# Products of attention chances and values for two steps at a time, over a ring of six pairs of chances

## The reference

```
h = layernorm(x) * (1 + ca) + sa
q, k, v = split(h @ W_qkv.T + b_qkv)            # 16 heads of 16
scores = q k^T * 16**-0.5, causal (-inf above the diagonal)
attn = softmax(scores); out = attn @ v; x = x + ga * (out @ W_out.T + b_out)
h = layernorm(x) * (1 + cb) + sb
cw = group-limited top-4 weights of softmax(h @ gate_w.T)   # 16 experts
x = x + gb * (sum_e cw[:, e] * swiglu_e(h) + swiglu_shared(h))
```

## Time and profile before

| what | us |
|---|---|
| median of 3 runs | 717.92 (717.07 to 720.73) |
| the profiled execution's own time | 718.91 |
| its span, first to last instruction | 716.9 |
| TensorE busy over the span | 626.2 (87%) |
| VectorE busy | 523.8 (73%) |
| ScalarE busy | 392.6 (55%) |
| GpSimd busy | 321.3 (45%) |
| products L2005 busy | 83.6, 768 matmuls |
| first score to last product | 94.9 to 397.7 |

### The profile page before, as it was taken

The page is one execution under the profiler, slowest core; times in us unless marked ns, Lnnn a source line. Parts: engine busy times, 40 slices in busy tenths (PEclk is TensorE's granted clock), DMA queues, the critical chain, the costliest instruction groups (busy, mean ns, idle before and its releaser), DMA issues. The chain is left out here.

```text
span 716.9 us, 13724 instructions
## 1 busy us (share of the span) xinstructions
PE 626.2 (87%) x3946; PEld 412.2 (58%) x3946; DVE 523.8 (73%) x1466; ACT 392.6 (55%) x919; POOL 321.3 (45%) x511
## 2 busy tenths in 40 slices
PE   2959879898999998978977989778999999999967
PEld 2747433334343434443423767567778888888756
DVE  4899978878788786857775687857886556555558
ACT  4446256666666656555686544436855455555440
POOL 4535533616142225327187874714973343434400
PEclk9979879999999999977999899989999999999979
DMA  8249957713030403032042435728333333333277
GB/s 277 90 141 277 351 165 203 198 37 105 16 99 23 119 2 100 21 128 105 31 148 76 147 129 189 248 88 288 103 105 121 105 107 120 107 120 107 75 300 299
DMA packets 65020, 98.03 MB, mean 137 GB/s; under 512 B 12115, under 2 KB 49747, under 8 KB 64693
## 3 DMA queue, kind: packets, MB, share of 16 engines
q1 hardware_dynamic: 56788, 73.10, 33.1%
q0 software_dynamic: 6864, 19.01, 7.0%
q10 hardware_dynamic: 1296, 5.05, 2.0%
HBM read 52.77 MB, written 42.14 MB: 132 GB/s over the span
## 5 line engine op out<-in xcount | busy, mean ns | idle before, releaser
L1261 ACT ACTIVATE Pr<-bank 128x512 f32<-128x512 f32 (+3 forms) x384 | 166.2, 494 | 99.3 <-PE bank L2019 94.2
L2019 PE MATMUL bank<-Qs,Ks 99*128 99x512 bf16 (+3 forms) x384 | 123.6, 344 | 16.0 <-ACT Pr L1261 10.4
L1915 PE MATMUL bank<-Ks,Qs 96*128 96x512 bf16 (+3 forms) x384 | 126.4, 348 | 6.5 <-DVE mxB L1382 5.3
L1382 DVE TENSOR_REDUCE mxA<-bank 128x1 f32<-128x128 f32 (+3 forms) x256 | 113.0, 485 | 25.4 <-PE bank L1915 24.9
L1094 POOL DMA_INDIRECT expert_rows<-Y,YIX x79 | 77.0, 975 | 116.3 <-DVE YIX L1802 84.2
L1078 POOL TENSOR_TENSOR tick<-ident 128x1 f32<-128x1 f32 x128 | 26.2, 204 | 179.3 <-ACT Pr L1261 178.7
L1382 DVE TENSOR_REDUCE mxB<-bank 128x1 f32<-128x512 f32 x128 | 82.0, 683 | 17.0 <-PE bank L1915 16.5
L2239 PE MATMUL bank<-W,xh 128*128 x316 | 84.3, 349 | 3.4 <-issue 3.4
L2005 PE MATMUL bank<-Pr,Vst 128*32 128x512 f32 (+3 forms) x768 | 83.6, 508 | 2.4 <-POOL Pr L1080 2.4
L1047 POOL DMA_INDIRECT chosen_rows<-Hx,pos x64 | 68.2, 1066 | 27.4 <-issue 17.6
L2019 PEld LDWEIGHTS bank<-Qs,Ks 99*128 99x128 bf16 x384 | 36.9, 100 | 71.8 <-ACT Pr L1261 44.4
(11 more groups left out here) (247 smaller groups left out, 1356.0 us busy)
## 6 DMA issues: line engine op xcount, KB each, us to landing
G<-chosen_rows SPq DMA_DIRECT2D x79, 132.0 KB, 2.1
Z<-expert_rows SPq DMA_DIRECT2D x16, 512.0 KB, 10.0
Wraw<-in_wexp SPq DMA_DIRECT2D x11, 608.0 KB, 5.1
qk_parts<-AP SPq DMA_DIRECT2D x16, 384.0 KB, 5.0
Qs<-qk_parts SPq DMA_DIRECT2D x16, 384.0 KB, 4.5
Ks<-qk_parts SPq DMA_DIRECT2D x8, 768.0 KB, 9.1
qk_parts<-AP SPq DMA_DIRECT2D x16, 256.0 KB, 5.2
Vst<-Vall SPq DMA_DIRECT2D x8, 512.0 KB, 9.8
```

Source lines behind the costliest of these rows:

```text
L1261: nc.scalar.activation(Pr[(2 * s + j // 2) % 4][:, j % 2, 0:w], ebank[p % RING][:, 0:w], ACT.Exp, scale=SCALE).then_inc(exp_done, EXP)
L1382: nc.vector.tensor_reduce(dst, mbank[u % RING][:, 0:w], AX.X, ALU.max).then_inc(m_red, 1)
L1915: nc.tensor.matmul(mbank[u % RING][:, 0:w], Qs[slot][0:NPR, i // TPC, j, (i % TPC) * P:(i % TPC + 1) * P], Ks[slot][0:NPR, j, k0:k0 + w], ...
L2019: nc.tensor.matmul(ebank[p % RING][:, 0:CH - q0], Ks[slot][0:NAUG, j, kt * P:(kt + 1) * P], Qs[slot][0:NAUG, qc, j, q0:CH], start=True, st ...
```

## The change

`BATCH = 2`: behind the last score of each even step s come the products of steps s - 2 and s - 1, and behind those of step 0 of a group the products of steps 10 and 11 of the group before. The ring of chances grows from four pairs to `PR_SLOTS = 6`, three steps; the two new pairs lie in the area of `AP` behind A. ScalarE's exponentials of step s now wait for the products of step s - 3 (before: s - 2), and those of step 2 of group 0 wait until the parts in `AP` have left for DRAM. `Hx1` moves into the area of the loads G; its wait for the parts goes. `out` of the second half moves from the end of step 3 to the end of step 2. The wait for the maxima's parts moves from ahead of the products to directly ahead of `max`. In groups 4 and 5 `ta` and `pj` move one step later, with what ScalarE and VectorE do for them. SP's loads for a slot of the queries' ring wait for the last product of the group before instead of the first of this one, and the load of expert words into places 14 and 15 waits for the last product instead of two stores.

```diff
+BATCH = 2
+PR_SLOTS = 2 * (BATCH + 1)
...
         if p % HG == PRODUCTS_AFTER:
-            order.append(("products", s - 1))
+            if s % BATCH == 0:
+                for k in range(BATCH):
+                    order.append(("products", s - BATCH + k))
             if s == 1:
                 order.append(("max", 1))
-            if s == 3:
+            if s == 2:
                 order.append(("out", 1))
...
 LATE_PE = {
-    (4, 2): [("ta", 0, 0)], (4, 3): [("ta", 0, 1)], (4, 4): [("pj", 0, 0)], (4, 6): [("pj", 0, 1)],
-    (5, 2): [("ta", 1, 0)], (5, 3): [("ta", 1, 1)], (5, 4): [("pj", 1, 0)], (5, 6): [("pj", 1, 1)],
+    (4, 3): [("ta", 0, 0)], (4, 4): [("ta", 0, 1)], (4, 5): [("pj", 0, 0)], (4, 7): [("pj", 0, 1)],
+    (5, 3): [("ta", 1, 0)], (5, 4): [("ta", 1, 1)], (5, 5): [("pj", 1, 0)], (5, 7): [("pj", 1, 1)],
...
 UNIT_DVE = {
-    (4, 22): [("res", 0, 0)], (4, 34): [("res", 0, 1)], **{(4, 36 + t): [("stats", 0, t)] for t in range(TPC)},
-    **{(4, 41 + t): [("aggr", 0, t)] for t in range(TPC)}, (4, 45): [("vars", 0)], (5, 24): [("res", 1, 0)],
...
+    (4, 28): [("res", 0, 0)], (4, 37): [("res", 0, 1)], **{(4, 38 + t): [("stats", 0, t)] for t in range(TPC)},
+    **{(4, 42 + t): [("aggr", 0, t)] for t in range(TPC)}, (4, 46): [("vars", 0)], (5, 28): [("res", 1, 0)],
...
+        for i in range(4, PR_SLOTS):
+            Pr.append(nc.alloc_sbuf_tensor_at(f"Pr{i}", [P, 2, CH], F32, offset=att0 + ATT + NIT * CH * 4 + (i - 4) * 2 * CH * 4))
...
+        Hx1 = nc.alloc_sbuf_tensor_at("Hx1", [P, TPC, ROWW], F32, offset=late.at)
...
-                    for c in (1, 3):
-                        sp.wait_ge(xs_out[c], 16 * TPC * TOPK)
+                    sp.wait_ge(pv_done, NIT * NS)
...
-                    sp.wait_ge(pv_done, n * NS + 1)
+                    sp.wait_ge(pv_done, n * NS)
...
-                        if j == 0 and not (n == 0 and s < 2):
-                            act.wait_ge(pv_done, n * NS + (s - 1))
-                        nc.scalar.activation(Pr[(2 * s + j // 2) % 4][:, j % 2, 0:w], ebank[p % RING][:, 0:w],
+                        if j == 0 and not (n == 0 and s < BATCH + 1):
+                            act.wait_ge(pv_done, n * NS + (s - BATCH))
+                        if n == 0 and s == BATCH and j == 0:
+                            for i in range(2):
+                                act.wait_ge(parts_out[i], 16 * 12 * B)
+                        nc.scalar.activation(Pr[(2 * s + j // 2) % PR_SLOTS][:, j % 2, 0:w], ebank[p % RING][:, 0:w],
...
                     if what == "products":
-                        if i == 0:
-                            turn_max_waits(n, 1)
-                        if i == 5 and not last:
-                            turn_max_waits(n + 1, 0)
                         if i >= 0:
                             products(n, slot, i)
                         elif n:
-                            products(n - 1, at(-1)[0], NS - 1)
+                            products(n - 1, at(-1)[0], NS + i)
                     if what == "max" and (i == 1 or not last):
+                        turn_max_waits(n + 1 - i, i)
                         turn_max()
...
-            products(NIT - 1, (NIT - 1) % SLOTS, NS - 1)
+            for s in range(NS - BATCH, NS):
+                products(NIT - 1, (NIT - 1) % SLOTS, s)
```

More of the change, by code:

```diff
@@ L105 @@
 PRODUCTS_AFTER = HG - 1
+BATCH = 2
+PR_SLOTS = 2 * (BATCH + 1)
+assert NS % BATCH == 0 and 2 * NS % PR_SLOTS == 0
 def masked_before(s):
@@ L174 @@
 LATE_ACT = {
-    (4, 3): [("ta", 0, 0)], (4, 4): [("ta", 0, 1)], (5, 0): [("root", 0)], (5, 3): [("ta", 1, 0)],
-    (5, 4): [("ta", 1, 1)], (5, 10): [("h", 0, 0)], (5, 11): [("h", 0, 1)],
+    (4, 4): [("ta", 0, 0)], (4, 5): [("ta", 0, 1)], (5, 0): [("root", 0)], (5, 4): [("ta", 1, 0)],
+    (5, 5): [("ta", 1, 1)], (5, 10): [("h", 0, 0)], (5, 11): [("h", 0, 1)],
     (6, 1): [("exp", 0)], (6, 0): [("root", 1), ("load", 0), ("load", 1), ("load", 2)],
@@ L200 @@
 UNIT_DVE = {
-    (4, 22): [("res", 0, 0)], (4, 34): [("res", 0, 1)], **{(4, 36 + t): [("stats", 0, t)] for t in range(TPC)},
-    **{(4, 41 + t): [("aggr", 0, t)] for t in range(TPC)}, (4, 45): [("vars", 0)], (5, 24): [("res", 1, 0)],
-    (5, 34): [("res", 1, 1)], **{(5, 36 + t): [("stats", 1, t)] for t in range(TPC)},
-    **{(5, 41 + t): [("aggr", 1, t)] for t in range(TPC)}, (5, 45): [("vars", 1)], (6, 1): [("soft", 0)],
+    (4, 28): [("res", 0, 0)], (4, 37): [("res", 0, 1)], **{(4, 38 + t): [("stats", 0, t)] for t in range(TPC)},
+    **{(4, 42 + t): [("aggr", 0, t)] for t in range(TPC)}, (4, 46): [("vars", 0)], (5, 28): [("res", 1, 0)],
+    (5, 37): [("res", 1, 1)], **{(5, 38 + t): [("stats", 1, t)] for t in range(TPC)},
+    **{(5, 42 + t): [("aggr", 1, t)] for t in range(TPC)}, (5, 46): [("vars", 1)], (6, 1): [("soft", 0)],
     **{(6, 5 + i): [("route", 0, 1 + i, 2 + i)] for i in range(23)},
@@ L376, in program @@
             "p (q t n d) -> p q t n d", n=NIT, q=S // CH, t=TPC)
-        Hx1 = nc.alloc_sbuf_tensor_at("Hx1", [P, TPC, ROWW], F32, offset=att0 + ATT + NIT * CH * 4)
-        assert NIT * CH * 4 + TPC * ROWW * 4 <= 2 * 3 * 4 * CH * 2
+        for i in range(4, PR_SLOTS):
+            Pr.append(nc.alloc_sbuf_tensor_at(f"Pr{i}", [P, 2, CH], F32, offset=att0 + ATT + NIT * CH * 4 + (i - 4) * 2 * CH * 4))
+        assert NIT * CH * 4 + (PR_SLOTS - 4) * 2 * CH * 4 <= 2 * 3 * 4 * CH * 2
         OT = [outs.put(f"OT{i}", [P, CH], F32) for i in range(2)]
@@ L442, in program @@
         late = Area(att0 + NW * EW * 4, early0 + EARLY - att0 - NW * EW * 4)
+        Hx1 = nc.alloc_sbuf_tensor_at("Hx1", [P, TPC, ROWW], F32, offset=late.at)
+        assert GRING >= TPC
         G = [late.put(f"G{i}", [P, ROWW], F32) for i in range(GRING)]
@@ L708, in rows_waits @@
                 eng.wait_ge(xs_out[c - 2], 16 * TPC * TOPK)
-            if c == 1 and t == 0:
-                for i in range(2):
-                    eng.wait_ge(parts_out[i], 16 * 12 * B)
         def attention(body):
@@ L1078, in body @@
                             nc.gpsimd.tensor_tensor(tick[:, k:k + 1], ident[:, 0:1], ident[:, 0:1], ALU.mult)
-                            v = Pr[(2 * s + pair) % 4][:, :, 0:P]
+                            v = Pr[(2 * s + pair) % PR_SLOTS][:, :, 0:P]
                             nc.gpsimd.affine_select(out=v, in_=v, compare_op=ALU.is_ge, fill=0.0, base=0,
@@ L2005, in products @@
                     ins = nc.tensor.matmul(pvb[32 * j:32 * j + 32, q0:CH], Vst[slot][:, kt, 32 * j:32 * j + 32],
-                                           Pr[(2 * s + j // 2) % 4][:, j % 2, 0:w],
+                                           Pr[(2 * s + j // 2) % PR_SLOTS][:, j % 2, 0:w],
                                            start=(kt == 0), stop=(kt == TPC * (qc + 1) - 1), skip_group_check=True)
```

## The result

| | before | changed |
|---|---|---|
| median, first chip | 717.92 us (9 runs: 714.43 to 720.73) | 723.62 us (9 runs: 720.28 to 728.33) |
| ratio, first chip | | 1.0084 (95%: 1.0053 to 1.0115) |
| span and clock of the profiled execution | 716.9 us, 0.945 | 721.8 us, 0.939 |
| median, second chip | 720.10 us (20 runs) | 721.65 us (12 runs), ratio 1.0031 (1.0003 to 1.0060) |

The change is a small loss, 0.8% on one chip and 0.3%, barely clear of noise, on another. Some executions of a kernel run at a lower granted clock and take longer; the ratios leave those out on both sides, so a ratio isn't the quotient of the two medians. The forecast of 719.4, 1.5 us over the kernel before, is 4.2 us low on the first chip. On the second the change costs 1.55 us by the medians; as will be seen, that agreement is luck, since the parts don't add up as I had them.

What follows compares the result with a forecast made beforehand. TensorE was taken as the bound until group 6, nothing in group 7. Terms 0.5 + 3.0 - 2.2 + 0.2 - 0.8 = +0.7, with +0.8 for the clock +1.5: 720.4 profiled, 719.4 by the median; range 709 to 729.

Steps and rivals of the forecast that it cites:

- The saving: TensorE's switch into and out of products, 0.24 us, is paid once per pair of steps: 48 batches, 11.5 us less.
- Rival D: The second step's products pay the switch again: saving 0, waits stay, +11.5 us, 731; chance 0.06.
- The cover, undisturbed group: Groups 1 to 3: TensorE waits +2.4 us on VectorE without products between units, less 1.4 of switches: +1.0 each.
- Unit 19 in groups 1 and 2: Steps 3 and 4: `normalise` leaves VectorE's chain, P2 and `out` leave the cover; the wait grows 0.6 to 0.8, taken 0.6.
- Group 0: No products of a group before, no `out` in step 3 to lose as cover, first chain as before: +0.5 us.
- Groups 4 and 5: Late work fills TensorE's holes; `ta` and `pj` no longer wait 0.92 and 0.40: -1.1 us each, -2.2.
- Group 7: Scores' added waits for ScalarE's exponentials, 1.4, equal the 1.4 saved; `ta` of chunk 2 stops waiting 0.79: -0.8 us.
- The clock: Half clock behind TensorE's wait in group 1 (and 2) costs 1.7 us; one half of one more such stretch: +0.8.
- Rival C: More and closer TensorE waits make the clock fall again and again: four more stretches of 1.7 us, 726; chance 0.09.
- Behind the last products: The part after group 7's last products: no change, 0.
- Rival B: Rings of three banks decide everywhere, late work or not; `ta` still waits 0.9: +8.6 us, 726.5; chance 0.18.

Runs made afterwards that it cites:

- the half-width experiment: VectorE's row maxima read half of the columns, in both kernels: kernel before 731.14 us (0.9867), changed kernel 731.66 us (0.9876).
- the bias edit: GpSimd's eight bias additions moved from steps 4-7 of groups 1, 2 to steps 8-10 of groups 0-2: changed kernel 713.23 us (0.9925), kernel before 741.10 us (0.9942).
- single products: Changed kernel with the products of each step made behind the next step again, one at a time, the rest kept: 752.08 us, ratio 1.0143.
- the fastest: Kernel before with pairs, early `out` and moved `ta` and `pj` in groups 4 and 5 alone, and GpSimd's bias additions moved: 707.58 us, ratio 0.9818.
- the two edits of the kernel before: Kernel before with row maxima over half the columns (731.14 us, 0.9867); kernel before with late work of groups 4 and 5 moved alone (746.02 us, 0.9937).

## Why the prediction was right or wrong, point by point

- **The saving** of 0.24 per pair: right (0.86 for a second step). Rival D is out.
- **The cover, undisturbed group**: right, +1.2 for +1.0, each wait within 0.2 us of its forecast, and the half-width experiment shows the cause. Missed: 0.2 twice where two scores now stand together.
- **Unit 19 in groups 1 and 2: the first mis-sized term.** I took +0.6 from group 3 for all; measured +1.56 (2.28 to 3.84), twice. The step that was wrong is that `normalise` leaves VectorE's chain and so shortens it. In group 3 it does: from unit 15 to unit 19 pass 2.99 us instead of 3.40. In groups 1 and 2 they are 6.03 instead of 5.44, with pairs and with single products alike, since the parts, now behind `normalise`, start later and have three stretched operations beside the additions instead of two. TensorE's own work in that time, the cover, falls by 1.0 (5.44 - 2.28 to 6.03 - 3.84). I had the row and used it for the clock only. That is 1.9 of the miss.
- **Group 0**: +1.0 for +0.5. Unit 19 waits 0.5 more (1.06 to 1.54), which I had put at nothing; but the changed kernel with the bias edit, whose unit 19 waits as long (1.49), takes 32.94 at the clock of before (0.94), so the +1.0 is nearly all clock (0.91). On the second chip the kernel before is the longer one there (35.16 against 34.07).
- **Groups 4 and 5**: right in sign, undervalued (-1.7 and -2.2 for -1.1 each). `ta` and `pj` wait no more than the plain 0.2, the answer to the earlier trace rows:

```profile
247.29 0.66 PE L2041 MATMUL bank<-ident,AP 128*128 128x128 f32 x4
...
253.44 1.97 PE L2053 MATMUL bank<-Wog,AT 128*128 128x256 f32 x8
...
381.31 0.87 PE L2041 MATMUL bank<-ident,AP 128*128 128x128 f32 x6
```

  By the experiments 1.8 of it is `out` early together with the late work moved to suit it, and next to nothing the pairs. The moved late work alone gives nothing; `out` early alone wasn't run.
- **Group 7: the step that failed.** Forecast -0.8, measured +1.6. `ta` gained what was said (0.79 to nothing in the row above). But I priced the cover of ScalarE by its exponentials alone. Its late pieces lie between them. Timeline of ScalarE and TensorE after:

```profile
369.46 1.00 ACT L1214 ACTIVATE W<-Wraw 128x960 fp32r<-128x960 f32 x1
...
374.97 1.06 ACT L1230 ACTIVATE XH<-SX 128x1024 fp32r<-128x1024 f32 x1
```

```profile
371.55 1.03 PE L2028 MATMUL bank<-Qs,Ks 99*128 99x512 bf16 x3 [0.63 <-ACT Pr L1270]
...
376.57 1.58 PE L2028 MATMUL bank<-Qs,Ks 99*128 99x512 bf16 x3 [0.88 <-ACT Pr L1270]
...
386.08 1.35 PE L2028 MATMUL bank<-Qs,Ks 99*128 99x512 bf16 x3 [0.39 <-ACT Pr L1270]
```

  Behind a piece of 1.0 us, scores that had products ahead of them now stand (scores 17, 25 and 33: 0.80, 1.04, 0.55). In sum the scores' waits rose from 8.8 to 12.0 us. Score 16 has a new one too, 1.0 by the profile for a transfer of the queries; in the kernel with the bias edit it is 0.2 and score 17's 1.6, so the sum of the two, 1.8, is ScalarE's either way. About 0.7 of the 2.1 lost up to score 31 is that, the rest the clock and P10 of group 6; 0.5 came back behind it.
- **The clock.** TensorE's stretches at 1.2 GHz moved. Two of them after: behind the long wait of group 1, and the longer one in group 2, in which TensorE is busy 4.36 of 6.80.

```profile
145.40:148.80 3.40, 3.40 (x29) 1.76 (x18) 2.32 (x7) 1.77 (x3) 0.00 (x0) 0.50 0.44 131
179.50:186.30 6.80, 4.36 (x29) 2.14 (x30) 5.18 (x11) 1.75 (x3) 2.97 (x3) 0.50 0.65 173
```

  Groups 6 and 7 before, then after, rows as above (PEclk is the third number from the end):

```profile
310.31:359.45 49.14, 40.79 (x265) 17.84 (x264) 31.75 (x95) 29.55 (x61) 18.88 (x43) 0.83 0.24 86
359.45:397.29 37.84, 27.94 (x197) 11.12 (x193) 24.71 (x76) 27.82 (x61) 29.68 (x54) 0.98 0.30 106
```

```profile
313.76:360.58 46.82, 38.07 (x264) 16.91 (x264) 30.71 (x95) 29.00 (x61) 18.98 (x43) 0.89 0.25 91
360.58:400.00 39.42, 31.57 (x201) 12.52 (x201) 24.01 (x74) 27.37 (x61) 28.44 (x55) 0.89 0.31 102
```

  Where TensorE is the bound, a length times (1 - PEclk) is what the clock costs: group 6 8.4 us before and 5.2 after, so its -2.3 is less clock, 3.2, and without it the group is 0.9 longer; the kernel before with the late work's new places alone has the same 0.89. Group 7 pays 0.8 and at most 4.3. Rival C (the clock falls again and again) is not what happened: group 3 with its new waits of up to 1.1 us kept 1.00. The rule that I weighed for it (the Trainium skill, "TensorE: Matmul & The Clock Gate", section "A second HAM failure mode: psum-queue depth-cycling") isn't borne out by those waits. That the clock can fall behind a wait of 1.4, group 2 with the bias edit shows.
- **Behind the last products** +2.2 for 0. On the second chip the same code took 318.4 in the kernel before, 321.9 in the changed one, 318.6 in that with the bias edit and 320.7 in the fastest. In the three profiles above 320 the second stretch at half clock there lasts 6.8 us (435.5 to 442.3 in the changed kernel), in the others 3.4. That can be 1.7 of it; the rest is open.
- **Rival B** (rings decide everywhere) forecast 726.5 and C 726; both are nearer to the total of the first chip than my 719.4, but B's condition, a `ta` that still waits 0.9, is false, and C's too, as said. On the profiled execution the miss is 3.4 (+4.9 for +1.5): groups 1 and 2 are 2.9 over their forecast, group 7 2.4 and the part behind 2.2, groups 4 to 6 are 4.2 under theirs, and the rest (0.9, less the 0.8 set for the clock) is small. That the sum came out within 1% is luck in so far as these cancel.

## What to carry to other kernels

Work that one engine does between its bursts of work for another is cover, and its worth is what the other engine gets done in that time: price it in each stage with the longest operation that stands there, not with the typical one. Saving 0.24 us a pair paid only where something else filled the hole, so make such a change per stage and not everywhere. And look for what stretches a chain before shortening it: eight additions on GpSimd cost this kernel more (0.6%) than the whole change moved on the second chip.

## What the runs showed of the hardware that I had not expected

- VectorE operations on 16 columns that take 0.17 to 0.32 us take 1.2 beside GpSimd additions of 1.23 each; row maxima from PSUM beside the same additions keep their 0.62. The Trainium skill, "SBUF — State Buffer", section "SBUF: two separate sides", says that GpSimd and a VectorE operation with two SBUF inputs shut each other out for a whole instruction; two of the three operations are of that kind and agree. The third, the cast, has one input and is stretched as well; the Trainium skill has the same, in that section, of an operation in a 2-port perf mode, and whether the cast ran in one no trace shows.
- Behind the wait of 3.7 us in groups 1 and 2 TensorE was granted 1.2 GHz for 3.4 and 6.8 us, though it was busy for 3.40 and 4.36 us of them. Without that wait both groups ran at 1.00 throughout in the kernel before with the bias edit and in the fastest; in the changed kernel with the bias edit group 2 did not (0.95).
- Chips differ: on two of four the kernel before took some 748 us instead of 718 to 720. In four of the eight kernels traced there score 35 of group 7 waited over 4 us, in the two edits of the kernel before with 38.3 us for the group 0.5.
